# Two layer norms in one, a layer norm without a centring product, chained layer norms, and a segment pipeline one unit deeper

## The chip, the core and the metric

The kernel runs on one core of one Trainium2 chip. A core has five engines with queues of their own: TensorE (PE, matrix products; PEld are its weight loads), VectorE (DVE), ScalarE (ACT), GpSimd (POOL) and SyncE (SP, which here only starts DMAs). Each works its queue in order and waits on semaphores for the others. The metric is the device time of the whole program in microseconds (us).

## What is computed

Eight layers over the same tensor of 4 x 1024 tokens of 128 features (all in f32), each added to its input behind a plain layer norm:

```python
x = x + rwkv_moe(layernorm(x))       # its own first step is again a layer norm: _ln(., ln1_g, ln1_b)
x = x + ffn(layernorm(x))            # ends in layernorm(x + collapsed, gamma, beta)
x = x + favor(layernorm(x))
x = x + ffn(layernorm(x))
x = x + segment_attention(layernorm(x))
x = x + tree(layernorm(x))
x = x + lru(layernorm(x))
x = x + tree(layernorm(x))

def _layernorm(x, axis=-1, eps=1e-05):
    m = jnp.mean(x, axis=axis, keepdims=True)
    v = jnp.var(x, axis=axis, keepdims=True)
    return (x - m) / jnp.sqrt(v + eps)
```

In the feed-forward layer each token picks one of nine paths by a small score; `x` in `x + collapsed` is the layer's normed input. In the segment attention a token attends to its own segment of 64 and to every fourth token of four neighbouring segments.

## The kernel before

**Layout.** Features lie on the 128 partitions, the 4096 tokens on the free axis, cut in eight chunks (`NCH`) of 512 (`CH`). PSUM has eight banks of 128 x 512 f32 (`k.bank[0..7]`). The order on each engine is written out by hand, stage after stage. No scheduler moves anything.

**A layer norm** (class `Norm`, driven by `layernorm`) takes a chunk through five steps: `center` (PE, line 85: the product with `I - 1/128`, into bank c % 4), `square` (ACT, line 92), `variance` (PE, line 103: the mean over the partitions as a product, into banks 4 to 6, or 4 and 5 where `vary` is 2), `deviation` (ACT, lines 110 and 112: Ln, then Exp of minus one half), and `scale` (DVE: line 118 for a plain norm. With gain and bias it is 121 and 124, or 121 and 126 where the result is added to the residual). On PE the loop does `variance(c - 2)`, then `center(c)`, then whatever the stage feeds in. On ACT it does `square(c + 2)`, then `deviation(c)`. `center(c)` waits until `ln_out` shows that the chunk four back has been scaled, since it writes over that chunk's bank; the count runs on from norm to norm, so the next norm's chunk 0 waits for chunk 4 of this one.

**The start.** The input is loaded in rows, turned on PE (line 2224), copied to `X` by DVE (2178, the `keep` step), normed into `Y` (no gain), and normed again into `N` with `ln1_g` and `ln1_b`: two passes of eight chunks. The vectors of all layers arrive as rows in one small table, `vrows`, which PE turns at the end of the first pass and DVE copies to `vecs` (2248). POOL then folds three vectors into weights (192, 195), and `wkv` begins: its products (219, 220) on PE, copies out of PSUM on ACT (281), a scan on DVE (354).

**The feed-forward layer** (`feedforward`, called twice) takes chunk by chunk: `hidden` (PE 858, three products), `scores` (864), DVE's `choose` (804 to 812), `turned` (870), `spread` (878, the choice as three masks in banks 6, 7 and 4), DVE's `mask` (820), `down` (885, three products with `W2`) and DVE's `add` (825, the sum with the normed input, into `Z`). The last chunk's steps stand behind the loop, with three `center` products of the closing norm between them. Then comes that norm (gain, bias, residual, in place on `X`), and behind it the plain norm `X` to `Y` that begins the next layer. Only `center(0)` and `square(0)` of the second are drawn forward (`ahead`).

**The segment stage** (`segments`) works 64 units (`N`). For unit n: `scores` (PE 1830, into one of two pairs of banks), DVE's `maxima` (2009, 2010) and `shift` (2018, 2019), ACT's `exp` (1930), POOL's `halve` (1977), DVE's `sums` (2026, 2028), ACT's `weight` (1934, 1936), POOL's `weigh` (1982, 1983), PE's `turned` (1840), ACT's copy of it (1926), PE's `weighed` (1852). In PE's turn n stand `scores(n)`, `turned(n - 3)`, `weighed(n - 4)`, and then one of three things that share one bank, `other`: a `project` (1812), a `values` (1863) or an `output` (1870). Each waits (`free()`) until the last one's result was read out of `other`: by ACT for `project` (1908 or 1898) and `values` (1919), by DVE's `add` (2033, residual) for `output`. ACT's `heads` (1942) empties the bank of `weighed` every eight units. In each batch of 16 units `project` stands at 0, 1, 3, 4, 7 and 11, `values` at 2, 6, 10 and 14, `output` at 5 and 13 from unit 13 on.

## Time and profile before

| | us |
|---|---|
| median of three runs | 1274.57 |
| lowest and highest | 1271.35, 1275.83 |
| the profiled execution | 1270.62 |
| its span in the profile | 1268.9 |

| stretch of the span (us) | what runs |
|---|---|
| 0 to 46 | load, two layer norms |
| 46 to 424 | wkv, experts |
| 424 to 544 | feed-forward with its norms |
| 544 to 688 | favor |
| 688 to 809 | feed-forward with its norms |
| 809 to 1084 | segment attention |
| 1084 to 1269 | tree, lru, tree, store |

All times below count from the start of the span; 1.7 us of the run lie outside it. A row of the timeline gives the start, the time from start to end, and in brackets how long the engine had been idle and who ended that. Neighbouring instructions overlap a little, so the step from one start to the next is often less than the duration. An f32 product shows as two PE instructions. In a row of stretches PEclk is the clock granted to TensorE as a share of 2.4 GHz; its two levels are 2.4 and 1.2 GHz, so that 0.57 is a mix of both.

### The profile page before, as it was taken

Reading aid. Unit: us, or ns where it says so; the run is one execution under the profiler, and the core shown is the slowest. Engines: PE = TensorE matmul, PEld = TensorE weight load, DVE = VectorE, ACT = ScalarE, POOL = GpSimd, SP = SyncE. Lnnn points to the kernel's source line nnn. Section 1 sums busy time; section 2 is a strip of 40 time slices with the busy share of each in tenths; the row PEclk is TensorE's granted clock in tenths of the full one; section 3 lists DMA queues with packets and bytes.
Section 4 is the critical chain, followed back from the end, with each engine's and each line's share of the span. In section 5 each row is a group of like instructions: output and inputs, shape, how many; then the busy total and the mean of one; then the engine's idle time right before and its main releaser. Section 6 shows DMA issues by size and latency. Waiting matters only on the chain.

```text
span 1268.9 us, 20399 instructions
## 1 busy us (share of the span) xinstructions
PE 1153.0 (91%) x7516; PEld 637.1 (50%) x7516; DVE 923.8 (73%) x1508; ACT 831.1 (65%) x1324; POOL 207.0 (16%) x313
## 2 busy tenths in 40 slices
PE   8988899999999999889998899798989888898787
PEld 4333344444444344367765353366666666463345
DVE  3869688777777756557775675488999997477766
ACT  5868655565565744745576636667787876768684
POOL 1000000000000000000000000167778777000000
PEclk9999999999999989979999999878999999999899
DMA  6000112212121000000000000000000000000002
GB/s 168 1 1 0 46 58 67 62 59 67 59 63 62 8 1 0 10 1 2 2 1 1 1 0 9 1 1 2 2 2 3 9 7 2 10 0 1 0 1 67
DMA packets 26076, 27.16 MB, mean 21 GB/s; under 512 B 3885, under 2 KB 17024, under 8 KB 25984
## 3 DMA queue, kind: packets, MB, share of 16 engines
q1 hardware_dynamic: 25938, 25.92, 6.9%
q8 instruction: 59, 0.97, 0.3%
q14 instruction: 33, 0.27, 0.1%
q10 hardware_dynamic: 46, 0.01, 0.0%
HBM read 23.30 MB, written 2.62 MB: 20 GB/s over the span
## 4 chain that ended last, share of the span: by engine, by line
PE 61%; DVE 16%; ACT 13%; issue 7%; POOL 1%; DMA 0%; DVEq 0%; ACTq 0%
PE psum L655 8%; PE psum L644 8%; PE psum L85 5%; PE psum L647 4%; PE psum L885 3%; PE psum L858 3%; PE psum L1830 3%; PE psum L1499 3%; ACT ln_std L112 3%; ACT ln_std L110 2%; PE psum L103 2%; PE psum L1273 2%; DVE arena L2010 2%; DVE N L2019 2%; ACT ln_sq L92 2%
## 5 line engine op out<-in xcount | busy, mean ns | idle before, releaser
L683 ACT ACTIVATE arena<-psum 128x512 f32<-128x512 f32 x128 | 69.5, 594 | 112.9 <-PE psum L644 112.9
L644 PE MATMUL psum<-arena,weights 128*128 128x512 f32 x256 | 120.8, 594 | 1.7 <-DVE N L124 1.0
L655 PE MATMUL psum<-arena,weights 128*128 128x512 f32 x256 | 120.3, 592 | 0.0
L103 PE MATMUL psum<-ln_sq,mean 128*128 128x512 f32 x192 | 97.1, 600 | 2.8 <-ACT ln_std L110 1.5
L541 DVE SCALAR_TENSOR_TENSOR arena<-diff,vecs,N 128x512 f32<-128x512 f32 x128 | 95.2, 746 | 0.0
L1930 ACT ACTIVATE N<-N 128x1024 f32<-128x1024 f32 x64 | 67.8, 1059 | 38.3 <-DVE N L2019 37.8
L603 DVE SCALAR_TENSOR_TENSOR arena<-arena,psum 128x512 f32<-128x512 f32 x64 | 44.0, 688 | 61.1 <-PE psum L655 61.1
L92 ACT ACTIVATE ln_sq<-psum 128x512 f32<-128x512 f32 x96 | 56.1, 593 | 45.5 <-PE psum L85 45.5
L1840 PE MATMUL psum<-ident,N 128*128 128x128 f32 x512 | 72.7, 287 | 12.5 <-POOL N L1983 11.9
L1830 PE MATMUL psum<-arena 32*128 32x128 f32 x1024 | 78.8, 295 | 4.8 <-ACT arena L1898 4.8
L1830 PEld LDWEIGHTS psum<-arena 32*128 32x128 f32 x1024 | 66.1, 197 | 31.3 <-issue 14.8
L655 PEld LDWEIGHTS psum<-arena,weights 128*128 128x128 f32 x256 | 48.6, 190 | 61.2 <-issue 61.2
L644 PEld LDWEIGHTS psum<-arena,weights 128*128 128x128 f32 x256 | 48.0, 190 | 62.0 <-issue 57.6
L1926 ACT ACTIVATE arena<-psum 128x1024 f32<-128x1024 f32 x64 | 65.5, 1024 | 17.8 <-PE psum L1840 17.6
L85 PE MATMUL psum<-X,center 128*128 128x512 f32 x128 | 67.4, 621 | 4.9 <-DVE N L118 1.9
L110 ACT ACTIVATE ln_std<-psum,eps 128x512 f32<-128x512 f32 x96 | 65.2, 679 | 8.9 <-PE psum L103 8.9
L118 DVE TENSOR_TENSOR Y<-psum,ln_std 128x512 f32<-128x512 f32 x48 | 33.2, 692 | 51.1 <-ACT ln_std L112 51.1
L1840 PEld LDWEIGHTS psum<-ident,N 128*128 128x128 f32 x512 | 57.2, 145 | 22.4 <-POOL N L1983 16.4
L694 ACT ACTIVATE arena<-arena 128x1024 f32<-128x1024 f32 x64 | 68.3, 1067 | 0.0
L1983 POOL TENSOR_TENSOR N<-N,arena 128x512 f32<-128x512 f32 x64 | 67.7, 1058 | 0.0
L1982 POOL TENSOR_TENSOR N<-N,arena 128x512 f32<-128x512 f32 x64 | 66.7, 1043 | 2.1 <-ACT arena L1936 2.1
L647 PE MATMUL psum<-arena,weights 128*128 128x512 f32 x128 | 65.4, 592 | 0.0
(318 smaller groups left out, 2452.2 us busy)
## 6 DMA issues: line engine op xcount, KB each, us to landing
arena<-tw_rows SPq DMA_DIRECT2D x64, 256.0 KB, 3.2
out_dram<-arena SPq DMA_DIRECT2D x8, 256.0 KB, 3.6
arena<-in_L_attn_a_x_dram SPq DMA_DIRECT2D x3, 512.0 KB, 6.4
weights<-in_L_attn_a_eWk_dram SPq DMA_DIRECT2D x1, 1024.0 KB, 5.9
arena<-in_L_attn_a_x_dram SPq DMA_DIRECT2D x2, 256.0 KB, 3.3
weights<-in_L_attn_a_eWr_dram SPq DMA_DIRECT2D x1, 512.0 KB, 9.6
tw_rows<-arena SPq DMA_DIRECT2D x2, 128.0 KB, 2.7
tw_rows<-arena SPq DMA_DIRECT2D x1, 256.0 KB, 3.7
```

The lines of the kernel that those rows point to most:

```text
L85: self.nc.tensor.matmul(k.bank[c % W][:], k.center[:], self.src(c), start=True, stop=True).then_inc(k.ln_centered, 1)
L92: self.nc.scalar.activation(k.ln_sq[:, c % W, :], k.bank[c % W][:], ACT.Square).then_inc(k.ln_squared, 1)
L103: self.nc.tensor.matmul(k.bank[W + c % self.vary][:], k.mean[:], k.ln_sq[:, c % W, :], start=True, stop=True).then_inc(k.ln_var, 1)
L110: self.nc.scalar.activation(k.ln_std[:, c % W, :], k.bank[W + c % self.vary][:], ACT.Ln, bias=k.eps[:, 0:1]).then_inc(k.ln_logs, 1)
L541: op = nc.vector.scalar_tensor_tensor(mixed[:, n % 4, a, :], k.diff[:, q % 2, :], k.vec((f"cm_k{e}", f"cm_r{e}")[a]), before, ALU.mult, AL ...
L644: op = nc.tensor.matmul(k.bank[2 * (n % 2) + h][:], k.eWk[:, e, h * P:(h + 1) * P], mixed[:, n % 4, 0, :], start=True, stop=True)
L647: nc.tensor.matmul(k.bank[6][:], k.eWr[:, e, :], mixed[:, n % 4, 1, :], start=True, stop=True).then_inc(k.ex_r, 1)
L655: op = nc.tensor.matmul(k.bank[4 + n % 2][:], k.eWv[:, e, h, :], ks[:, (2 * (n % 2) + h) * CH:(2 * (n % 2) + h + 1) * CH], start=(h == 0), ...
L683: op = nc.scalar.activation(kr[:, h * CH:(h + 1) * CH], k.bank[2 * (n % 2) + h][:], ACT.Relu)
L694: nc.scalar.activation(ks[:, n % 2 * 2 * CH:(n % 2 + 1) * 2 * CH], kr, ACT.Square).then_inc(k.ex_sq, 1)
L1830: op = nc.tensor.matmul(scored[half][:, e * P:(e + 1) * P], k.sg_Q[b % 2][at, seg, 2 * j:2 * j + 2, :].rearrange("p h n -> p (h n)"), k.sg ...
L1840: op = nc.tensor.transpose(turned_to[:, e * P:(e + 1) * P], pr[n % 4][:, e * P:(e + 1) * P], k.ident[:])
```

## The change

**1. The first two norms in one** (`TwoNorms`). After the first norm the features of a token have mean zero and variance v / (v + eps), so the second norm's factor is `(v (1 + eps) + eps^2)^(-1/2)` of the same centred value. There is one pass instead of two: PE centres and takes the variance once, ACT does two Ln and two Exp from the same bank, and DVE writes both `N` (with gain, then bias) and `Y`. `ln1_g` and `ln1_b` leave the table of rows and are loaded by themselves as columns, 128 x 1 each, first on ACT's queue. The table is turned in PE's turn 5 and copied after chunk 3 of the pass.

**2. The closing norm of the feed-forward layer without centring** (`CentredNorm`). The rows of `W2` (with `b2`) are made mean-free once, by DVE at the end of the norm ahead of the first feed-forward layer (two reductions, two small and three 128 x 128 operations), so `Z` has mean zero by itself. POOL squares each chunk of `Z` when `add` has written it. PE takes the mean of that into one of the banks 0, 1, 2, 0, 6, 7, 4, 5, and DVE scales from `Z` in SBUF. `center` and `square` are gone.

**3. The pair chained.** The next norm's `center(c)` for the first four chunks waits only for chunk c of the closing norm. Three of its `center` and two of its `square` stand inside the closing pass.

**4. Segments.** `turned` and `weighed` come one unit later on PE and ACT, `output`, `heads` and DVE's `add` too, `values` one unit earlier, and one `project` at 2 instead of 1.

```diff
+class TwoNorms(Norm):
+    def deviation(self, act, c):
...
+        act.wait_ge(k.ln_var, self.n0 + c + 1)
+        var = k.bank[W + c % self.vary][:]
+        nc.scalar.activation(k.ln_std[:, at, :], var, ACT.Ln, bias=k.eps[:, 0:1])
+        nc.scalar.activation(k.ln_std2[:, at, :], var, ACT.Ln, scale=1.0 + EPS_LN, bias=k.eps_eps[:, 0:1]).then_inc(k.ln_logs, 1)
+        act.wait_ge(k.ln_logs, self.n0 + c + 1)
+        nc.scalar.activation(k.ln_std[:, at, :], k.ln_std[:, at, :], ACT.Exp, scale=-0.5)
+        nc.scalar.activation(k.ln_std2[:, at, :], k.ln_std2[:, at, :], ACT.Exp, scale=-0.5).then_inc(k.ln_rstd, 1)
+    def scale(self, dve, c):
...
+        nc.vector.scalar_tensor_tensor(out, bank, k.ln1[:, 0:1], k.ln_std2[:, at, :], ALU.mult, ALU.mult).then_inc(k.ln_scaled, 1)
+        nc.vector.tensor_tensor(self.dst(c), bank, k.ln_std[:, at, :], ALU.mult)
+        dve.wait_ge(k.ln_scaled, self.second0 + c + 1)
+        nc.vector.tensor_scalar(out, out, k.ln1[:, 1:2], None, ALU.add).then_inc(k.ln_out, 1)
+class CentredNorm(Norm):
+    SPOTS = (0, 1, 2, 0, 6, 7, 4, 5)
+    def variance(self, pe, c):
...
+        pe.wait_ge(k.ff_sq, self.squared0 + c + 1)
+        self.enter(pe, c)
+        self.nc.tensor.matmul(k.bank[self.SPOTS[c]][:], k.mean[:], self.squares(c), start=True, stop=True).then_inc(k.ln_var, 1)
+    def scale(self, dve, c):
...
+        nc.vector.scalar_tensor_tensor(self.src(c), self.src(c), k.vec(self.gain), k.ln_std[:, c % W, :], ALU.mult, ALU.mult).then_inc(k.ln_scaled, 1)
+        nc.vector.scalar_tensor_tensor(self.residual(c), self.src(c), k.vec(self.bias), self.residual(c), ALU.add, ALU.add).then_inc(k.ln_out, 1)
...
-        pe.wait_ge(k.ln_out, self.n0 + c + 1)
+        pe.wait_ge(k.ln_out, self.n0 + c + 1 - (self.chained if c < W else 0))
...
+        if self.chained and c < W:
+            act.wait_ge(k.ln_out, self.n0 + c + 1)
...
+        for c in range(NCH):
+            pool.wait_ge(k.ff_z, PRIMED["ff_z"] + base + c + 1)
+            nc.gpsimd.tensor_tensor(after.squares(c), after.src(c), after.src(c), ALU.mult).then_inc(k.ff_sq, 1)
...
+        after.scale(dve, 0)
+        after.scale(dve, 1)
         mask(B - 1, 1)
+        add(B - 1, 0)
+        after.scale(dve, 2)
         add(B - 1, 1)
...
-    PROJ = {0: 0, 1: 1, 3: 2, 4: 3, 7: 4, 11: 5}
+    PROJ = {0: 0, 2: 1, 3: 2, 4: 3, 7: 4, 11: 5}
...
-        return n // 4 if n < N and n % 4 == 2 else None
+        return n // 4 if n < N and n % 4 == 1 else None
...
-        return (n - 13) // 8 if n >= 13 and n % 8 == 5 else None
+        return (n - 14) // 8 if n >= 14 and n % 8 == 6 else None
...
-            if 0 <= n - 3 < N:
-                turned(n - 3)
             if 0 <= n - 4 < N:
-                weighed(n - 4)
+                turned(n - 4)
+            if 0 <= n - 5 < N:
+                weighed(n - 5)
```

**ACT in the first pass.** Before: squares, then one Ln and one Exp for a chunk (the pass follows twice in this form).

```order
L92 ACTIVATE ln_sq<-psum 128x512 x3
L110 ACTIVATE ln_std<-psum,eps 128x512
L112 ACTIVATE ln_std<-ln_std 128x512
L92 ACTIVATE ln_sq<-psum 128x512
L110 ACTIVATE ln_std<-psum,eps 128x512
L112 ACTIVATE ln_std<-ln_std 128x512
```

Now, once (`eps_eps` is the constant eps squared, `arena` here holds the second factor):

```order
L94 ACTIVATE ln_sq<-psum 128x512 x3
L149 ACTIVATE ln_std<-psum,eps 128x512
L150 ACTIVATE arena<-psum,eps_eps 128x512
L152 ACTIVATE ln_std<-ln_std 128x512
L153 ACTIVATE arena<-arena 128x512
L94 ACTIVATE ln_sq<-psum 128x512
L149 ACTIVATE ln_std<-psum,eps 128x512
```

A chunk has four such operations and a square instead of, over both passes, four and two squares; the dependent passes have become one.

**PE at the end of the feed-forward layer.** Before: from behind the last `scores` (L864) over three `center` of the closing norm to its first `variance`.

```order
L85 MATMUL psum<-arena,center 128x512
L870 MATMUL psum<-ident,arena 9x128 x4
L85 MATMUL psum<-arena,center 128x512
L878 MATMUL psum<-arena,spread 128x512 x3
L85 MATMUL psum<-arena,center 128x512
L885 MATMUL psum<-arena,ffw 128x512 x3
L133 UNCONDITIONAL_BRANCH
L103 MATMUL psum<-ln_sq,mean 128x512 x2
```

Now, from the same place (L192 is the variance of the closing norm, L87 the next norm's `center`, from `X`):

```order
L192 MATMUL psum<-arena,mean 128x512 x2
L974 MATMUL psum<-ident,arena 9x128 x4
L990 MATMUL psum<-arena,ffw 128x512 x3
L982 MATMUL psum<-arena,spread 128x512 x3
L192 MATMUL psum<-arena,mean 128x512 x2
L990 MATMUL psum<-arena,ffw 128x512 x3
L219 UNCONDITIONAL_BRANCH
L192 MATMUL psum<-arena,mean 128x512
L87 MATMUL psum<-X,center 128x512
L192 MATMUL psum<-arena,mean 128x512
L87 MATMUL psum<-X,center 128x512
```

Four variances now stand ahead of the last `down`, and the two norms alternate behind it.

**PE in the segment stage, units 13 to 16.** Before: `output`, then the turns of 14 (with `values`), 15 and 16 (with `project`).

```order
L1870 MATMUL psum<-arena,weights 128x512
L1830 MATMUL psum<-arena 128x128 x8
L1840 MATMUL psum<-ident,N 128x128 x8
L1852 MATMUL psum<-arena,ln_sq 32x64 x16
L1863 MATMUL psum<-ident,arena 128x128 x4
L1830 MATMUL psum<-arena 128x128 x8
L1840 MATMUL psum<-ident,N 128x128 x8
L1852 MATMUL psum<-arena,ln_sq 32x64 x16
```

Now, from `values` in turn 13 (L1970) to the end of turn 15: L1937 is `scores`, L1947 `turned`, L1959 `weighed`, L1977 `output`.

```order
L1970 MATMUL psum<-ident,arena 128x128 x4
L1937 MATMUL psum<-arena 128x128 x8
L1947 MATMUL psum<-ident,N 128x128 x8
L1959 MATMUL psum<-arena,ln_sq 32x64 x16
L1977 MATMUL psum<-arena,weights 128x512
L1937 MATMUL psum<-arena 128x128 x8
L1947 MATMUL psum<-ident,N 128x128 x8
L1959 MATMUL psum<-arena,ln_sq 32x64 x16
```

Behind `output` there was a `values` one turn later; now the next user of `other` is the `project` of turn 16, or of turn 7 in a batch that has one there.

## Rows read from the trace of the kernel before

**Rows 1.** Page, part 1: busy us, share of the span, instructions.

```profile
PE 1153.0 (91%) x7516; PEld 637.1 (50%) x7516; DVE 923.8 (73%) x1508; ACT 831.1 (65%) x1324; POOL 207.0 (16%) x313
```

**Rows 2.** Stretches: us, busy us by engine (instructions), PEclk, DMA share, GB/s.

```profile
12.00:46.00 34.00, 31.84 (x85) 13.52 (x84) 18.29 (x33) 28.45 (x49) 3.14 (x14) 1.00 0.33 91
500.00:546.00 46.00, 38.07 (x96) 15.35 (x95) 25.00 (x47) 30.32 (x51) 1.88 (x11) 1.00 0.03 7
820.00:840.00 20.00, 16.63 (x84) 10.95 (x84) 14.08 (x25) 10.10 (x19) 6.93 (x9) 0.57 0.00 1
840.00:1076.00 236.00, 204.48 (x3544) 158.50 (x3544) 213.05 (x370) 186.49 (x348) 181.92 (x208) 0.98 0.02 4
```

**Rows 3.** Timeline: ACT in the first two passes, and DVE's first scan.

```profile
13.05 0.68 ACT L110 ACTIVATE ln_std<-psum,eps 128x512 f32<-128x512 f32 x1
...
22.92 0.58 ACT L92 ACTIVATE ln_sq<-psum 128x512 f32<-128x512 f32 x1
...
23.40 0.68 ACT L110 ACTIVATE ln_std<-psum,eps 128x512 f32<-128x512 f32 x1
24.11 0.63 ACT L112 ACTIVATE ln_std<-ln_std 128x512 f32<-128x512 f32 x1
...
24.65 0.67 ACT L110 ACTIVATE ln_std<-psum,eps 128x512 f32<-128x512 f32 x1
...
43.91 0.63 ACT L112 ACTIVATE ln_std<-ln_std 128x512 f32<-128x512 f32 x1
...
47.13 2.29 DVE L354 TENSOR_TENSOR_SCAN arena<-diff,arena 128x1024 f32<-128x1024 f32 x1 [0.16 <-ACT arena L281]
```

**Rows 4.** Timeline, second pass: from a factor to the square four chunks on.

```profile
30.98 0.63 ACT L112 ACTIVATE ln_std<-ln_std 128x512 f32<-128x512 f32 x1
...
31.65 0.75 DVE L121 SCALAR_TENSOR_TENSOR N<-psum,vecs,ln_std 128x512 f32<-128x512 f32 x1 [3.59 <-ACT ln_std L112]
...
32.44 0.49 DVE L124 TENSOR_SCALAR N<-N,vecs 128x512 f32<-128x512 f32 x1
...
34.14 0.60 ACT L92 ACTIVATE ln_sq<-psum 128x512 f32<-128x512 f32 x1 [0.80 <-PE psum L85]
```

**Rows 5.** Timeline: end of both feed-forward layers, first scale of the second norm.

```profile
499.22 1.05 PE L864 MATMUL psum<-Wo,arena 64*128 64x9 f32 x8
...
506.59 2.74 PE L885 MATMUL psum<-arena,ffw 128*128 128x512 f32 x6
...
529.57 0.69 DVE L118 TENSOR_TENSOR Y<-psum,ln_std 128x512 f32<-128x512 f32 x1 [1.84 <-ACT ln_std L112]
...
796.98 0.69 DVE L118 TENSOR_TENSOR Y<-psum,ln_std 128x512 f32<-128x512 f32 x1 [1.84 <-ACT ln_std L112]
```

**Rows 6.** Page, part 5: a product of two 128 x 512 tiles on POOL.

```profile
L1982 POOL TENSOR_TENSOR N<-N,arena 128x512 f32<-128x512 f32 x64 | 66.7, 1043 | 2.1 <-ACT arena L1936 2.1
```

**Rows 7.** Timeline, inside the feed-forward loop: DVE's mask.

```profile
461.78 1.88 DVE L820 TENSOR_TENSOR arena<-arena,psum 128x512 f32<-128x512 f32 x3 [0.57 <-PE psum L878]
```

**Rows 8.** Timeline, segment stage: units 18 to 20 and 23, and what preceded.

```profile
895.92 0.69 DVE L2009 TENSOR_REDUCE arena<-psum 128x8 f32<-128x512 f32 x1
...
899.37 0.68 DVE L2009 TENSOR_REDUCE arena<-psum 128x8 f32<-128x512 f32 x1
...
899.93 1.12 ACT L1919 ACTIVATE ln_sq<-psum,weights 128x128 f32<-128x128 f32 x4
...
903.37 0.69 DVE L2009 TENSOR_REDUCE arena<-psum 128x8 f32<-128x512 f32 x1 [0.48 <-PE psum L1830]
...
914.59 0.66 PE L1863 MATMUL psum<-ident,arena 128*128 128x128 f32 x4 [1.76 <-DVE X L2033]
...
916.38 0.69 DVE L2009 TENSOR_REDUCE arena<-psum 128x8 f32<-128x512 f32 x1 [0.93 <-PE psum L1830]
```

**Rows 9.** Waits of 820 to 1076: total us, times, longest.

```profile
DVE arena L2009 <- PE psum L1830: 23.0, 30, 3.4
```

**Rows 10.** Timeline, end of the segment stage: the last `weighed`.

```profile
1081.44 0.65 PE L1852 MATMUL psum<-arena,ln_std 128*32 128x64 f32 x32
```

More of the change, by code:

```diff
@@ L165, in first @@
     def first(pe, c):
-        if c == NCH + 1:
-            after.center(pe, 0)
+        if 6 <= c < 9:
+            after.center(pe, c - 6)
     def turned(act, c):
-        if c == NCH - 2:
-            after.square(act, 0)
+        if c in (5, 6):
+            after.square(act, c - 5)
     return first, lambda dve, c: None, turned
@@ L703, in stage_rwkv @@
 def stage_rwkv(nc, k, block, a, feed, norms):
-    first, second, third, after = norms
+    first, second, after = norms
     layernorm(k, block, first, feed)
@@ L707, in stage_rwkv @@
     ffn_loads(k, block, a)
-    layernorm(k, block, second)
-    wkv(nc, k, block, a, third)
-    experts(nc, k, block, lambda feed: layernorm(k, block, third, feed), after)
+    wkv(nc, k, block, a, second)
+    experts(nc, k, block, lambda feed: layernorm(k, block, second, feed), after)
 FFN_GROUPS = ((0, 2), (2, 6), (6, 9))
@@ L832, in turn @@
                 choose(it, c)
-                if not (first and c == 0):
+                if not (first and c == 0 or last and c == 1):
                     add(*before)
@@ L886, in down, with turn @@
             op.then_inc(k.ff_out, 1)
-        def turn(it, first):
+        def turn(it, first, last=False):
             for c in range(2):
@@ L901, in turn @@
                 scores(it, c)
-                if not (first and c == 0):
+                if not (first and c == 0 or last and c == 1):
                     down(*before)
         turn(0, True)
-        with pe.Fori(1, B) as it:
+        with pe.Fori(1, B - 1) as it:
             turn(it, False)
-        for c in range(3):
-            pe.wait_ge(k.ff_hid, 3 * (base + NCH - 1) + c + 1 + PRIMED["ff_hid"])
-            after.center(pe, c)
-            if c == 0:
-                turned(B - 1, 1)
-            if c == 1:
-                spread(B - 1, 1)
+        turn(B - 1, False, True)
+        after.variance(pe, 0)
+        after.variance(pe, 1)
+        turned(B - 1, 1)
+        down(B - 1, 0)
+        spread(B - 1, 1)
+        after.variance(pe, 2)
+        after.variance(pe, 3)
         down(B - 1, 1)
@@ L944, in _ @@
         activations(act, k, "natural_log_exp_and_others")
-        after.square(act, 0)
+        after.deviation(act, 0)
         choice(B - 1, 1)
-        for c in range(1, 3):
-            after.square(act, c)
+        for c in range(1, 4):
+            after.deviation(act, c)
 def stage_ffn(nc, k, block, norms):
@@ L954, in stage_ffn @@
     k.ff_calls += 1
+    after.chained = NCH - W
     feedforward(nc, k, block, call, lambda feed: layernorm(k, block, first, feed), second)
@@ L1948, in _ @@
                 queries(k.bank[4 + c], 0, c, part)
-        for n in range(N + 6):
-            if n >= 12 and n % 8 == 4:
-                heads((n - 12) // 8)
-            if 0 <= n - 3 < N:
-                turned(n - 3)
+        for n in range(N + 7):
+            if n >= 13 and n % 8 == 5:
+                heads((n - 13) // 8)
+            if 0 <= n - 4 < N:
+                turned(n - 4)
             if n < N:
@@ L2046, in _ @@
                 shift(n)
-            if n >= 14 and n % 8 == 6:
-                add((n - 14) // 8)
+            if n >= 15 and n % 8 == 7:
+                add((n - 15) // 8)
             if n >= 1:
```

148 lines of the change are left out of this document (112 added, 36 removed).

## The prediction

> **What bounds the kernel now.** I read the page's busy line first [rows 1]: PE is busy 91% of the span, so no other engine can be the bound everywhere, but the average hides stages with other limits. So I went on to the stretches [rows 2]. From 12 to 46 us, PE is busy 31.8 of 34.0 us and ACT 28.5. In the pair of norms after a feed-forward layer (500 to 546) it is 38.1 and 30.3 of 46. In the segment stage (840 to 1076) DVE has 213.1 of 236.0 and PE 204.5. In the norm passes no engine is full: each chunk runs PE, ACT, PE, ACT, DVE, and the bank that it holds comes free at the end. There I followed the timeline from one chunk to the next [rows 3 to 5]. In the segment stage I followed DVE's first reduction from unit to unit and read what it waited for [rows 8, 9].
>
> **Part 1, the first two norms in one.** In the pass of before, ACT takes 0.48 us from a square to the Ln behind it (22.92 to 23.40), 0.71 from Ln to the Exp that needs it (to 24.11) and 0.54 to the next instruction [rows 3]. Of two Ln in a row none shows the step; I take 0.57, between the square's 0.48 and the full 0.68. A chunk on ACT is then 0.48 + 0.57 + 0.71 + 0.54 + 0.54 = 2.84 us. The bank's cycle is longer. Before, an Exp ends at 30.98 + 0.63 = 31.61 and the square that waits for this chunk's bank (through DVE's 121, 124 and a `center`) starts at 34.14: 2.53 us [rows 4]. DVE now has one more operation between these two. Before, 124 starts 0.79 behind 121, since it needs its result; now two steps between independent operations lie there. Three masks take 1.88 us, so such a step is 0.60 [rows 7]; the one with gain is longer by 0.06, so I take 0.67 + 0.61. That is 0.49 more, 3.02 us. From that square to the end of the second Exp it is 0.48 + 0.57 + 0.71 + 0.54 + 0.63 = 2.93, so two chunks take 5.95. The first Ln stays at 13.05 [rows 3], and its factors end at 15.5. By the cycle the factors of chunks 1 to 5 end near 18.3, 21.4, 24.3, 27.4 and 30.3. The last two chunks need no square and take 2.36 each, so the last ends at 35.0. Before it was 43.91 + 0.63 = 44.54 [rows 3]. DVE's last scale is now 0.5 us longer and stands ahead of its first scan, so the scan gains 9.1 instead of 9.5: from 47.13 to 38.0. PE's first products of `wkv` wait for POOL's fold. The vectors are copied behind chunk 3, near 24.3 + 2 us, and the fold is POOL's 3.1 us of that stretch [rows 2], so they start near 30, with 5 us to spare. The two 128 x 1 loads have no like in the trace. They can cost nothing or, in front of the first input load, up to 1 us; I take 0.5. **Part 1: 8.6 us, bounds 6 and 10.**
>
> **Parts 2 and 3, the pair of norms.** PE's last `scores` start at 499.22 and are through at 500.2 [rows 5]. From there PE has, in order, two variances (0.86 each: the six instructions at 506.59 take 2.74, that is 0.43 apart), `turned` 0.43, `down` 2.58, `spread` 0.65, two variances and `down`: 9.7 us, ending at 509.95. Before, the last `down` began at 506.59 [rows 5] and was through 2.58 us later, so this piece is 0.8 us longer. DVE's two scales ahead of `mask` (1.5 us each) fit, since `mask` waits for `spread` anyway. POOL needs 1.04 us for a square, by its products of the same size [rows 6]. The last but one is there long before its variance; the last is ready near 512. Then PE alternates variance and `center`, seven products of 0.86 to 516.0. ACT with 1.25 us for a chunk (0.71 + 0.54) and two squares between ends its last factor at 517.6. Then come `square(2)`, Ln and Exp of the next norm's chunk 0, to 519.3, and DVE's first `scale` of that norm starts at 519.35. Before it was 529.57 [rows 5]: 10.2 us. From there on the second norm has the same steps and the same bank cycle as before. The second feed-forward layer has the same times shifted by 267.4 us (529.57 and 796.98 [rows 5]), so it gains the same. The fold of `W2` is seven DVE operations of a quarter or half of 128 x 512, at most 7 x 0.25 us by the 0.69 of a whole one. DVE then waits for the first `scores` of the layer, which covers them, so I cost the fold at nothing; without that cover it costs 1.7 us once. **Parts 2 and 3: 20.4 us, bounds 12 and 23.** The lower bound is the removed work alone, 0.86 us of PE for seven centrings a pass, without the chaining.
>
> Inside the feed-forward loop POOL's square runs beside DVE's mix of the next chunk. In the trace of before DVE has a wait of 0.57 us ahead of `mask` there [rows 7], and a product of `down` takes 0.86 us against 0.60 for a mask, so a late start of the masks is partly caught up. Even if a square held DVE up by its whole 1.04 us, most of it would fall into these gaps.
>
> No row shows what a POOL product does to a DVE operation with two inputs in SBUF. The Trainium skill, SBUF — State Buffer, section SBUF: two separate sides, says that the two engines share a pair of ports as an exclusive lock, taken by a DVE operation with two SBUF inputs against a POOL operation that reads SBUF. By it a square and the mix, or a square and a scale of the closing norm, would run one after the other.
>
> **Part 4, the segments.** With nothing to wait for, a unit takes DVE 3.45 us (895.92 to 899.37 [rows 8]). DVE waits for `scores` 23.0 us in all, 3.4 of it at the first unit [rows 9]: 19.6 us are there to be had. Two kinds make up most of it. Seven times the wait is 0.93 (at unit 23 [rows 8], and at 15, 31, 39, 47, 55 and 63): PE holds a `values` until DVE's `add` has read `other` (1.76 us idle at 914.59), and the next `scores` are queued behind it. The other kind follows a `values` copied by ACT (899.93 to 901.05 [rows 8]): the `project` of the next turn waits for it, and `scores` come 0.48 late (903.37); with ACT's `heads` there too I count 0.6. After the change `output` stands one turn later and the next user of `other` two or more turns on, except in the two batches where `project` stands at 7 right behind it (units 23 and 39). There the wait stays and gets longer by the difference of a `project` (0.86 and its filling, say 1.1) and a `values` (0.66 [rows 8]), to about 1.4 us. At the other five the 0.93 goes, but `values` now stands one turn ahead of each of the seven `output`, so 0.5 comes in its place. I count for after: 7 x 0.5 before `output`, 2 x 0.5 where `project` follows `values` at 17 and 33, 2 x 0.6 with `heads`, 2 x 1.4, and about 4 in the first 16 units, where the clock was 0.57 in the stretch 820 to 840 [rows 2]: 12.5 us against 19.6, so 7.1. Waits of PE for POOL before `turned` go too, but they only matter through these. At the end the last `weighed` starts at 1081.44 [rows 10], after two `center` of the next norm. These now come ahead of it, since ACT's copy is late anyway; 1.3 us. One price is new: DVE's `shift(n)` now waits for `turned(n - 4)` of the same turn. Four transposes take 0.66 us [rows 8], so the eight of `turned` end about 1.2 us after `scores(n)`, and `shift` starts behind two reductions of 0.68, 1.3 after them. At half clock it would be late by about 0.8 us a unit. **Part 4: 8.3 us, bounds 0 and 12.**
>
> **The sum.** 8.6 + 20.4 + 8.3 = 37.3. Against the profiled execution that is 1270.6 - 37.3 = 1233.3. That run lies 4 us under the median of the three, so for a median I predict **1237 us**, 2.9% less. A measurement here tells apart about 0.3%.
>
> **The rivals.** (a) *The deeper segment pipeline gives nothing*: the wait of `shift` for `turned`, and longer waits at `project`, eat part 4. For: DVE is 90% busy there, and only 0.1 to 0.3 us separate `turned` from `shift`. Against: five of the seven long waits lose their cause. It gives 1274.6 - 29.0 = 1246; chance 0.12. (b) *The pairs gain only the removed centring*: the chain then ends in ACT or DVE as before, with 12 instead of 20.4: also 1246; chance 0.08. (c) *POOL's squares hold DVE up*: 16 squares of 1.04 us [rows 6], none of them hidden, are 16.6 us: 1254. Against it are the gaps above; chance 0.08. This is the skill's rule on the shared ports carried to its end. (d) *Slower than before*: the segment stage falls to 1.2 GHz. PE's 204.5 us at 0.98 [rows 2] would take 401 us at half clock, so a us spent there loses about 0.4. Before, PE was at the low level for part of 820 to 840 only [rows 2]. With 120 us at the low level the loss is 49 and the time 1286. It decides from about 91 us on. The change leaves PE's work in the stage the same and its pauses shorter, so I give it 0.03. (e) *The merged norm is bound by something I don't see* (the column loads, the clock with a less busy PE): part 1 at 0 gives 1246; chance 0.05.
>
> **How the numbers follow.** The forecast as summed has 0.64. Its own bounds, with 4 us for where the clock's low stretches fall, are 1229 to 1243. The range must take in (a), (b) and (e), so it runs from 1228 to 1250 and leaves out (c), (d) and the low tail of the forecast. Faster by over 0.3%: all but (d), 0.97, of which I take 0.01 for cases that fall together; same 0.01, slower 0.03.
>
> **What would show it.** The first scan of `wkv` near 38 us and ACT without idle time before. The first plain scale 10 us earlier after each feed-forward layer, PE alternating variance and `center` without gaps. In the segment stage DVE's waits for `scores` about 12 to 13 us beyond the first one, none of 0.93 at units 15, 31, 47, 55 and 63, and long ones at 24 and 40. It would be wrong if DVE's mixes in the feed-forward loop took longer than before, if `shift` idled for `turned`, or if the low clock covered more of 820 onward.

## The result, and the profile after

The changed kernel takes **1257.0 us** (median of four executions; 1255.5 to 1258.7) against 1274.7 before (1271.4 to 1275.8, with a fourth execution beside the three above). The ratio is 0.9866, with a 95% interval from 0.984 to 0.989: 1.3% less, where I had forecast 2.9% (1237) and a range up to 1250. The profiled execution took 1258.3 us, with a span of 1256.2.

Of the page of after, the busy line (us, share of the span, instructions) and TensorE's granted clock in 40 slices; the first answers to [rows 1].

```profile
PE 1139.7 (91%) x7444; PEld 639.9 (51%) x7452; DVE 930.1 (74%) x1515; ACT 815.3 (65%) x1300; POOL 230.7 (18%) x330
...
PEclk9999999999999989989999999698899988999899
```

The changes ahead of the segments show in five rows of the timeline (start, duration): the scan, and in each feed-forward layer the first hidden product (L962) and the first plain scale (L122). They answer to the scan in [rows 3] and the first plain scales in [rows 5].

```profile
38.08 2.29 DVE L440 TENSOR_TENSOR_SCAN arena<-diff,arena 128x1024 f32<-128x1024 f32 x1
...
434.68 3.37 PE L962 MATMUL psum<-arena,ffw 128*128 128x512 f32 x6
...
512.84 0.69 DVE L122 TENSOR_TENSOR Y<-psum,ln_std 128x512 f32<-128x512 f32 x1 [0.18 <-ACT ln_std L116]
...
692.93 3.37 PE L962 MATMUL psum<-arena,ffw 128*128 128x512 f32 x6
...
769.84 0.69 DVE L122 TENSOR_TENSOR Y<-psum,ln_std 128x512 f32<-128x512 f32 x1 [0.19 <-ACT ln_std L116]
```

The first scan is 9.05 us earlier. From a layer's first hidden product to the first plain scale it takes 78.2 and 76.9 us. Before it took 88.4 and 87.2, from these products to the scales of [rows 5]:

```profile
441.15 1.02 PE L858 MATMUL psum<-arena,ffw 128*128 128x512 f32 x2
...
709.80 1.71 PE L858 MATMUL psum<-arena,ffw 128*128 128x512 f32 x3
```

Both pairs gained 10.3.

The segment stage shows the rest. First its stretches (columns as in [rows 2]; the last one runs from the first unit's maxima to the last unit's), then waits of 797 to 1053.7 (us in total, times, longest), the first of which answers to [rows 9].

```profile
795.00:815.00 20.00, 17.41 (x91) 11.31 (x92) 13.07 (x23) 7.89 (x18) 7.55 (x10) 0.50 0.00 0
815.00:1059.00 244.00, 215.06 (x3456) 167.34 (x3456) 212.54 (x369) 183.74 (x343) 177.89 (x204) 0.91 0.01 4
...
797.61:1053.64 256.03, 227.13 (x3451) 174.16 (x3452) 220.54 (x382) 188.02 (x353) 181.89 (x209) 0.88 0.01 4
```

```profile
DVE arena L2116 <- PE psum L1937: 31.2, 31, 3.4
...
PE psum L1959 <- ACT arena L2049: 9.9, 7, 2.4
PE psum L1947 <- ACT arena L2033: 7.3, 9, 1.7
...
DVE N L2125 <- PE psum L1947: 5.7, 9, 0.7
...
PE psum L1919 <- DVE X L2140: 3.5, 2, 1.8
```

TensorE's waits before, in the same stretch (824.8 to 1067.97), were longest for DVE's `add` and for GpSimd's weights:

```profile
PE psum L1863 <- DVE X L2033: 12.4, 7, 1.8
PE psum L1840 <- POOL N L1983: 10.1, 17, 1.2
PE psum L1852 <- ACT arena L1942: 4.1, 7, 1.1
```

DVE waits 31.2 us for scores where it waited 23.0, and 5.7 us more in its shift for `turned`. TensorE's waits for `add` fell from 12.4 us to 3.5, as meant, but all its waits in the stretch are 28.8 us in 29 times against 30.1 in 43: fewer, longer and for other engines. The mean granted clock is 0.88. Before, the same stretch was 243.2 us long with a granted clock of 0.96. At two levels, 0.88 over 256 us is about 61 us at 1.2 GHz; the clock records say 62.4, before 21.5.

The table takes each kernel apart, profiled executions all. "Low" is the time at 1.2 GHz in the stretch ahead of it, from the clock records. P is the start of the stage's first projections, D from the first unit's maxima to the last one's, tail from there to the last `add`, rest to the end of the span.

| kernel | median us | P | low | P to maxima | D | low | tail | rest |
|---|---|---|---|---|---|---|---|---|
| before | 1274.7 | 809.6 | 35.0 | 15.2 | 243.2 | 21.5 | 16.1 | 184.9 |
| after | 1257.0 | 782.4 | 41.9 | 15.2 | 256.0 | 62.4 | 17.3 | 185.3 |
| e1_turns_as_before | 1246.0 | 776.9 | 27.3 | 14.0 | 251.7 | 44.2 | 17.6 | 186.3 |
| e2_turns_alone | 1285.2 | 809.6 | 35.0 | 15.2 | 256.0 | 62.4 | 17.3 | 184.7 |
| e3_heads_first | 1247.2 | 780.0 | 38.5 | 15.2 | 248.7 | 58.9 | 17.3 | 185.1 |
| e4_centre_last | 1253.0 | 779.9 | 35.1 | 15.2 | 256.0 | 62.4 | 17.7 | 184.5 |
| e5_slots_alone | 1245.9 | 782.8 | 41.9 | 15.2 | 245.2 | 35.1 | 18.1 | 185.4 |
| e6_fill_start | 1250.1 | 779.7 | 34.1 | 11.4 | 254.4 | 54.6 | 17.3 | 184.7 |
| e7_heads_centres | 1247.9 | 776.9 | 31.7 | 15.2 | 249.2 | 55.5 | 15.6 | 186.4 |
| e8_squares_act | 1259.1 | 783.0 | 41.9 | 15.2 | 255.9 | 62.4 | 17.3 | 185.3 |
| e9_all_mended | 1231.4 | 779.7 | 34.1 | 11.4 | 239.2 | 17.1 | 14.0 | 184.8 |
| e10_fill_before | 1268.9 | 809.4 | 34.1 | 11.4 | 243.0 | 20.5 | 17.7 | 186.2 |
| e11_heads_centres | 1242.1 | 780.3 | 38.5 | 15.2 | 248.0 | 45.3 | 14.1 | 186.0 |
| e12_deep_mended | 1240.0 | 779.9 | 37.5 | 11.4 | 242.6 | 34.1 | 15.6 | 185.6 |

P varies by 5.9 us among the seven kernels whose code is the same up to there (after, e1, e3, e4, e5, e7 and e11: 776.9 to 782.8), and it roughly follows the low time ahead of it (27.3 to 41.9). Most of the spread lies between the first scan and the first hidden product: 392.3 us with none of it low in e7, 393.7 with 3.4 in e4, 396.6 with 10.2 in after; before it was 394.0 with 3.4. At an equal low time nothing is lost there, so the fold of `W2`, which the prediction costed at nothing, costs nothing. The sum predicted 809.6 - 29.0 = 780.6. The profiled run of after lies near the late end of that spread.

### The profile page after: what moved, and what is told of

It is laid out like the page before. It is cut to its first block, busy times and chain, and to the rows that moved or that the text cites. A ratio compares the mean times of both kernels' runs of the same rounds, so it can differ in the third digit from the quotient of the medians.

```text
span 1256.2 us, 20246 instructions
## 1 busy us (share of the span) xinstructions
PE 1139.7 (91%) x7444; PEld 639.9 (51%) x7452; DVE 930.1 (74%) x1515; ACT 815.3 (65%) x1300; POOL 230.7 (18%) x330
## 4 chain that ended last, share of the span: by engine, by line
PE 63%; DVE 17%; ACT 14%; issue 6%; DMA 0%; SPq 0%; DVEq 0%; ACTq 0%
PE psum L730 8%; PE psum L741 8%; PE psum L733 4%; PE psum L990 3%; PE psum L87 3%; PE psum L1937 3%; PE psum L962 3%; PE psum L1606 3%; PE psum L1947 2%; PE psum L1380 2%; DVE N L2126 2%; ACT ln_std L116 2%; ACT ln_std L114 2%; DVE arena L2117 2%; DVE arena L2116 2%
## 5 line engine op out<-in xcount | busy, mean ns | idle before, releaser
L1937 PE MATMUL psum<-arena 32*128 32x128 f32 x1024 | 84.6, 310 | 4.8 <-ACT arena L2005 4.8
L1937 PEld LDWEIGHTS psum<-arena 32*128 32x128 f32 x1024 | 71.1, 210 | 33.7 <-issue 18.7
L1947 PE MATMUL psum<-ident,N 128*128 128x128 f32 x512 | 77.2, 299 | 10.2 <-ACT arena L2033 9.9
L730 PEld LDWEIGHTS psum<-arena,weights 128*128 128x128 f32 x256 | 48.6, 192 | 62.4 <-issue 58.0
L105 PE MATMUL psum<-ln_sq,mean 128*128 128x512 f32 x144 | 73.2, 601 | 3.1 <-ACT arena L150 1.1
L87 PE MATMUL psum<-X,center 128*128 128x512 f32 x128 | 67.0, 618 | 6.5 <-DVE N L165 3.2
L1947 PEld LDWEIGHTS psum<-ident,N 128*128 128x128 f32 x512 | 61.2, 152 | 20.0 <-issue 15.1
L2116 DVE TENSOR_REDUCE arena<-psum 128x8 f32<-128x512 f32 x64 | 43.9, 687 | 31.3 <-PE psum L1937 31.2
L1775 DVE TENSOR_REDUCE arena<-psum 128x32 f32<-128x1024 f32 x32 | 39.2, 1224 | 32.8 <-PE psum L1606 32.8
L2084 POOL TENSOR_TENSOR mixed<-N 128x256 f32<-128x256 f32 x64 | 46.5, 727 | 74.4 <-ACT N L2037 74.3
## 6 DMA issues: line engine op xcount, KB each, us to landing
arena<-tw_rows SPq DMA_DIRECT2D x64, 256.0 KB, 3.1
out_dram<-arena SPq DMA_DIRECT2D x8, 256.0 KB, 3.6
arena<-in_L_attn_a_x_dram SPq DMA_DIRECT2D x2, 256.0 KB, 4.1
tw_rows<-arena SPq DMA_DIRECT2D x1, 256.0 KB, 3.4
```

Of the source, the lines that this page charges most:

```text
L87: self.nc.tensor.matmul(k.bank[c % W][:], k.center[:], self.src(c), start=True, stop=True).then_inc(k.ln_centered, 1)
L105: self.nc.tensor.matmul(k.bank[W + c % self.vary][:], k.mean[:], k.ln_sq[:, c % W, :], start=True, stop=True).then_inc(k.ln_var, 1)
L730: op = nc.tensor.matmul(k.bank[2 * (n % 2) + h][:], k.eWk[:, e, h * P:(h + 1) * P], mixed[:, n % 4, 0, :], start=True, stop=True)
L1937: op = nc.tensor.matmul(scored[half][:, e * P:(e + 1) * P], k.sg_Q[b % 2][at, seg, 2 * j:2 * j + 2, :].rearrange("p h n -> p (h n)"), k.sg ...
L1947: op = nc.tensor.transpose(turned_to[:, e * P:(e + 1) * P], pr[n % 4][:, e * P:(e + 1) * P], k.ident[:])
L2116: nc.vector.tensor_reduce(mx[n % 2][:, 0:8], mine, AX.X, ALU.max)
```

## Which part loses

**Part 4 taken out, and part 4 alone.** The edit of the first run, on the changed kernel (the second makes the same change, reversed, on the kernel before):

```diff
-            if 0 <= n - 4 < N:
-                turned(n - 4)
-            if 0 <= n - 5 < N:
-                weighed(n - 5)
+            if 0 <= n - 3 < N:
+                turned(n - 3)
+            if 0 <= n - 4 < N:
+                weighed(n - 4)
...
```

with `heads` and the turns of `project`, `values`, `output` and `add` as before.

> The changed kernel with the segment stage's turns put back as they were (part 4 undone, parts 1 to 3 kept). By the traces the stage starts 27.2 us earlier than before at its first maxima, and the store is only 13.3 earlier, so 13.9 us are lost behind it. If the new turns cause the loss (queue theory), units 0 to 63 take again the 243.2 us they took before and the tail its 16.0, and the time is 1275 - 27 = 1247 us, within 3; DVE's waits for the scores are again about 23 us in 30. If instead the loss comes from TensorE's clock in the earlier start, whatever the turns (clock theory), the stage stays at about 256 us and the time at 1255 to 1258.

> The kernel before with part 4 alone. Queue theory: 12.8 us more between the first and the last unit and 1.3 more in the tail, so about 1289 us (1284 to 1292), with the new wait for `turned` in DVE's shift and waits of some 2 us at units 14, 30, 46 and 62. Clock theory: the stage as before, or up to 8 us shorter as I predicted, 1266 to 1276 us.

Without part 4: **1246.0 us** (ratio 0.9765, 0.974 to 0.979). Part 4 alone: **1285.2 us** (1.0088, 1.006 to 1.011). Part 4 costs about 11 us on either base by the medians, and the executions of the kernels compared don't overlap (1241.8 to 1248.6 against 1255.5 to 1258.7, and 1283.9 to 1287.6 against at most 1277.0 beside them). Its stretch D is 256.0 us both times, with 62.4 us at the low clock both times, though it starts 27 us apart. So what falls low there goes with the order of the work more than with the place in time. But the order of before isn't fixed at 243.2 either: in e1 the same order took 251.7 us with 44.2 us low, and DVE waited 31.1 us in 37 for scores, where I expected 23 in 30. Its 22.7 us more of low clock cost 8.6, 0.38 for each. So in the profiled executions part 4 adds 12.8 us to D against the kernel before, but only 4.3 against e1: how large its loss is depends on the low clock in the kernel that it is set beside.

**The places alone.** The depth of three and four turns and `heads` as before, the new turns of `project`, `values`, `output` and `add` kept:

```diff
-            if 0 <= n - 4 < N:
-                turned(n - 4)
...
+            if 0 <= n - 3 < N:
+                turned(n - 3)
...
```

> The changed kernel with `turned` and `weighed` three and four turns behind as before, and `heads` where it was, but with the new turns of `project`, `values`, `output` and `add`. It splits part 4 in two: the run without part 4 took 1246 us, the changed kernel 1257. If the depth of the pipeline carries the loss (its `heads` standing behind the second half of `queries`), this kernel is at 1243 to 1248; if the new places of `project` and `values` carry it, at 1253 to 1258.

**1245.9 us** (0.9775, 0.975 to 0.981). The loss is in the depth, not in the places; but the places bring nothing by the medians either (e1: 1246.0), though they take the wait for `add` away here too (3.5 us in 2). D fell by 10.8 us to 245.2, with 35.1 us low (PEclk 0.93 in the row of its stretch), and TensorE again waits for GpSimd's weights, now its longest sum:

```profile
797.95:1043.13 245.18, 218.60 (x3491) 166.52 (x3492) 220.47 (x383) 189.34 (x354) 181.88 (x209) 0.93 0.01 4
```

```profile
PE psum L1947 <- POOL N L2090: 8.1, 12, 1.6
PE psum L1959 <- ACT arena L2049: 6.4, 5, 1.8
```

In after, the wait for GpSimd's weights is gone, as meant. But the transposes have one place in PSUM, so `turned` of one unit now waits for ACT's copy of the last one (7.3 us in 9), and `weighed` for `heads` (9.9 in 7, where it was 4.1 in 7 before).

## The queues

**`heads` behind `queries`.** In after, `weighed(8t + 8)` needs the bank that ACT's `heads` empties. TensorE's rows around unit 14, and ACT's:

```profile
847.59 1.06 PE L1947 MATMUL psum<-ident,N 128*128 128x128 f32 x8 [0.83 <-ACT arena L2033]
850.75 1.08 PE L1959 MATMUL psum<-arena,ln_sq 128*32 128x64 f32 x32 [2.10 <-ACT arena L2049]
851.76 1.12 PE L1970 MATMUL psum<-ident,arena 128*128 128x128 f32 x4
852.81 2.08 PE L1937 MATMUL psum<-arena 32*128 32x128 f32 x16
```

```profile
848.55 0.24 ACT L2043 ACTIVATE arena<-arena 128x40 f32<-128x40 f32 x1
848.69 1.43 ACT L2005 ACTIVATE arena<-psum,weights 128x512 f32<-128x512 f32 x2
850.01 0.59 ACT L2049 ACTIVATE arena<-psum 128x512 f32<-128x512 f32 x1
```

`heads` (L2049) stands behind the second half of `queries` (L2005, two copies, 1.43 us together). `weighed` idles 2.10 us, the scores queued behind it start late and at half clock (2.08 instead of 1.16 us), and DVE waits 3.43 us at unit 14. It waits 1.90, 2.14 and 1.94 at units 30, 46 and 62. TensorE waits 2.39 and 2.10 us for `heads` at 30 and 46, again behind `queries`. At 62 it waits 1.95, but there `heads` follows `exp` and `weight`, with no `queries` ahead: that wait is not explained by this order.

```diff
-            if n >= 13 and n % 8 == 5:
-                heads((n - 13) // 8)
...
             if 0 <= n - 1 < N:
                 weight(n - 1)
+            if n >= 12 and n % 8 == 4:
+                heads((n - 12) // 8)
```

> The changed kernel, with ScalarE's `heads` moved from the start of iteration 8t+13 to the end of iteration 8t+12, ahead of the second half of `queries`. If the waits of about 2 us at units 14, 30, 46 and 62 come from `heads` standing behind `queries` (queue theory), three of them (14, 30, 46: the last unit has no queries) lose 1.5 to 2 us each and the low clock that follows them, another 1 to 2 us each: 1247 to 1252 us. If they are only where the clock happens to be low, the time stays within 2 us of 1257.

**1247.2 us** (0.978, 0.975 to 0.982), 9.9 less than after by the medians. In the profile D is 7.3 us shorter with only 3.5 us less at the low clock, so some 6 us of it are the waits themselves. The units 14, 30 and 46 now wait 2.33, 0.96 and 0.96 us, and the sum behind `heads` fell from 9.9:

```profile
PE psum L1959 <- ACT arena L2049: 2.7, 4, 0.8
```

**The `center` products in the last turns.** After's end of the stage on TensorE:

```profile
1061.01 1.99 PE L87 MATMUL psum<-X,center 128*128 128x512 f32 x4
1062.83 1.04 PE L1947 MATMUL psum<-ident,N 128*128 128x128 f32 x8
...
1064.38 1.98 PE L87 MATMUL psum<-X,center 128*128 128x512 f32 x4
1066.20 1.04 PE L1947 MATMUL psum<-ident,N 128*128 128x128 f32 x8
```

Each pair of `center` (L87) holds a `turned` (L1947) for 1.8 us.

```diff
-            if n in (N + 1, N + 2):
-                pe.wait_ge(k.sg_arg, n - 2)
-                for c in range(2 * (n - N - 1), 2 * (n - N)):
+            if n in (N + 4, N + 5):
+                pe.wait_ge(k.sg_arg, n - 5)
+                for c in range(2 * (n - N - 4), 2 * (n - N - 3)):
```

> The changed kernel, with the two pairs of `center` of the next norm moved from TensorE's turns 65 and 66 to turns 68 and 69, behind the last `weighed`. In the changed kernel the last `turned` starts 12.6 us after the last maxima, before it was 10.0. Queue theory: the four products (1.0 to 1.2 us a pair, twice) no longer stand ahead of the last two `turned`, the last `add` comes 1.5 to 2.5 us earlier, about 1255 us. Rival: GpSimd's last weights are what the last `turned` waits for, and nothing changes (1257).

**1253.0 us** (0.983, 0.979 to 0.987), and no gain where I looked for it. The last `turned` starts 10.3 us after the last maxima instead of 12.6, but the `center` products now stand ahead of `output` (L1977), for which the last `add` waits; the tail is 17.7 us against 17.3:

```profile
1064.19 3.70 PE L87 MATMUL psum<-X,center 128*128 128x512 f32 x8
1067.72 1.02 PE L1977 MATMUL psum<-arena,weights 128*128 128x512 f32 x2
```

The median is 4 us lower, of which the profile shows 2.5 as an earlier P; its four executions spread over 9 us (1250.2 to 1259.0). So I put them where TensorE idles anyway:

```diff
+            if n == N:
+                pe.wait_ge(k.sg_arg, N - 1)
+                after.center(pe, 0)
+                after.center(pe, 1)
+            if n in (N + 1, N + 2):
+                pe.wait_ge(k.sg_arg, N)
+                after.center(pe, n - N + 1)
```

> The kernel with `heads` ahead of the second half of `queries` (1247.2 us), and with the next norm's four `center` spread over the last turns: two at turn 64, where TensorE waits 2.0 us for the copy of the turned unit, and one each at turns 65 and 66, where it waits 0.6. Queue theory: the last `turned` starts 10.3 us after the last maxima instead of 12.6 and the last `add` still 4.75 behind it, so 2.2 us less, 1245 us. Rival: the end of the stage is set by the chain of copies alone and the time stays at 1247.

**1247.9 us** (0.979, 0.975 to 0.984). The tail is 15.6 us instead of 17.3, near the 2.2 expected; the median can't tell that from e3's, whose runs spread over 8 us. That spread is wider than what this edit gives.

## The clock

TensorE waits 3.4 us ahead of the stage's first projections and 4.75 us behind them. In after the projections took 8.3 us, and units 0 to 4 ran at half clock. Idle products fill the two pauses, on the changed kernel and on the one before:

```diff
+        def fill(count):
+            for _ in range(count):
+                nc.tensor.matmul(other[:], k.center[:], k.X[:, 0:CH], start=True, stop=True)
...
             pe.wait_ge(k.sw_in, 7 * 16)
+            fill(3)
             pe.wait_ge(k.ln_out, normed)
...
         first()
+        fill(4)
```

> The changed kernel with idle products on TensorE, whose result nobody reads: three of 128x512 ahead of the segment stage's first projections, where TensorE waits 3.4 us, and four behind them, where it waits 4.75 us. Queue theory alone: the waits are covered by other work and nothing gets shorter, 1257 us (or up to 3 longer, if a filler still runs when its wait ends). Clock theory: the granted clock of the first projections and of units 0 to 8 stays at 2.4 instead of 1.2 GHz; the projections take 4.2 instead of 8.3 us and the units that wait for scores lose 1 to 1.5 us less each, 1245 to 1250 us.

> The kernel before with the idle products alone. Before, too, TensorE waits 3.4 us ahead of the stage's first projections and the clock is at 1.2 GHz in units 0 to 4. Clock theory: the first scores come 3 to 4 us earlier and 1 to 2 us of the first units' waits go, 1269 to 1271 us. If the idle products only shift the low stretches, 1273 to 1275.

**1250.1 us** (0.982, 0.978 to 0.985) and **1268.9 us** (0.9952, 0.994 to 0.997): 6.9 and some 6 us less. One of the six executions of e10 took 6426 us, which nothing here explains; without it the median is 1268.8. The rows of e6 (the idle products are L1911):

```profile
776.25 2.74 PE L1911 MATMUL psum<-X,center 128*128 128x512 f32 x6
779.72 5.42 PE L1918 MATMUL psum<-Y,weights 128*128 128x512 f32 x12 [0.74 <-DVE Y L122]
784.98 3.60 PE L1911 MATMUL psum<-X,center 128*128 128x512 f32 x8
789.90 1.16 PE L1942 MATMUL psum<-arena 32*128 32x128 f32 x16 [1.32 <-ACT arena L2011]
```

The six projections take 5.4 us, the first scores 1.16 instead of 2.08, and the first maxima come 11.4 us after P instead of 15.2. That is a gain from work that nobody needs. The rest of e6 lies in D (1.6) and ahead of P (2.7), which is the spread of P.

## The squares on GpSimd

In both closing norms ACT takes the squares of the last two chunks, where it idles, and GpSimd the other six:

```diff
-        for c in range(NCH):
+        for c in range(NCH - 2):
             pool.wait_ge(k.ff_z, PRIMED["ff_z"] + base + c + 1)
...
+    def own_square(self, act, c):
+        act.wait_ge(self.k.ff_z, self.z0 + c + 1)
+        self.nc.scalar.activation(self.squares(c), self.src(c), ACT.Square).then_inc(self.k.ff_sqa, 1)
```

> The changed kernel with the squares of the last two chunks of both feed-forward norms taken by ScalarE (which idles there) instead of GpSimd. In the changed kernel the two VectorE additions (both operands and result in SBUF) that run beside these squares took 1.41 us instead of 0.75. If that is a lock between the two engines, they take 0.75 again, and with VectorE on the path the time falls by 1.3 us a norm, 2.6 in all, 1254.5 us; if the additions are not on the path, 1257. If the lengthening has another cause, they stay at 1.41.

Rows of after, GpSimd's square and the two VectorE operations beside it, then the addition in e8:

```profile
501.88 0.74 DVE L210 SCALAR_TENSOR_TENSOR arena<-arena,vecs,ln_std 128x512 f32<-128x512 f32 x1
502.04 1.48 POOL L893 TENSOR_TENSOR arena<-arena 128x512 f32<-128x512 f32 x1 [11.05 <-DVE arena L925]
502.66 1.41 DVE L212 SCALAR_TENSOR_TENSOR X<-arena,vecs,X 128x512 f32<-128x512 f32 x1
```

```profile
503.17 0.75 DVE L220 SCALAR_TENSOR_TENSOR X<-arena,vecs,X 128x512 f32<-128x512 f32 x1
```

The addition is back at 0.75 us, so the 1.41 came from the square beside it. The median is **1259.1 us** (0.988, 0.983 to 0.993), no better than after, where 2.6 us less were expected. Its executions spread over 11 us, but the profile agrees: from the first hidden product to the first plain scale it takes 78.2 us as in after. Inside the feed-forward loop, too, the mixes beside a square took 1.22 us instead of 0.75, six of them in the first layer. They fell into VectorE's waits: the two pairs gained 10.3 us each all the same.

The Trainium skill, SBUF — State Buffer, section SBUF: two separate sides, says that the pair of ports goes to whichever of the two operations starts first, for its whole length. The trace agrees in both directions, if not to the full length: the square (1.04 us alone), begun 0.58 us before a scale's end, took 0.44 longer, and the addition, begun 0.86 before the square's end, took 0.66 longer.

## Everything mended, at either depth

The best version takes the places of part 4, the old depth, `heads` ahead of the first half of `queries` (iteration 8t + 11), the first three `center` in TensorE's wait of turn 64 with the fourth behind the last `weighed`, and the idle products; e11 leaves these out.

```diff
             if 0 <= n - 1 < N:
                 weight(n - 1)
+            if n >= 11 and n % 8 == 3:
+                heads((n - 11) // 8)
...
+            if n == N:
+                pe.wait_ge(k.sg_arg, N)
+                for c in range(3):
+                    after.center(pe, c)
+            if n == N + 3:
+                after.center(pe, 3)
```

> Parts 1 to 3, the new places of `project`, `values`, `output` and `add`, the old depth of three and four turns, and three more edits: `heads` at the end of iteration 8t+11, ahead of the first half of `queries`; the next norm's `center` of chunks 0 to 2 at the end of turn 64, where TensorE waits 2.7 us for GpSimd's weights, and that of chunk 3 behind the last `weighed`; and the idle products at the stage's start. From the run with the new places alone (1245.9 us): heads 1 to 2 us (0.9 us of wait at units 13, 29 and 45), the tail 4 us (the pairs of `center` took 3.5 and 2.0 us there ahead of turned(63) and weighed(63)), the idle products 5.4 us as they gained at the stage's start in their own run: 1235 us. If the clock takes its low stretches elsewhere instead, 1239 to 1242.

> The same without the idle products: 1240 to 1241 us by the queues alone (1245.9 less 4 in the tail and 1 to 2 for heads). If the tail's length is set by GpSimd's weights and not by the `center` products ahead of turned(63), 1244.

**1231.4 us** (0.968, 0.966 to 0.970) and **1242.1 us** (0.974, 0.973 to 0.976). Both are faster than the changed kernel; e9 is also faster than the run without part 4 (1246.0, 0.974 to 0.979), while e11's interval overlaps that one's. The tail is 14.0 and 14.1 us, 4 less than in e5, as expected. The idle products gave 10.7 us where I expected 5.4, since D shrank too: 239.2 us with 17.1 low against 248.0 with 45.3, that is 0.31 for each us at the low clock. The two profiled executions are e9's fastest and e11's slowest (1231.1 and 1245.6), so the profile shows more than the medians.

The twin of e9 at the changed kernel's depth is e7 with the idle products. It is no exact twin: its `heads` stands ahead of the second half of `queries`, and two `center` stand in turn 64 and one each in 65 and 66.

> The changed kernel at its own depth of four and five turns, with everything mended beside it: `heads` ahead of the second half of `queries`, the `center` products in TensorE's waits of the last turns, and the idle products at the stage's start. It asks whether the deeper pipeline is worth anything once nothing else is in its way; its twin at the old depth took 1231.4 us. My prediction's step (the depth shortens the waits for scores by 7 us) would give 1225 to 1228. If the depth brings nothing, 1230 to 1234. If the depth itself costs (the copy of the turned unit, the shift's wait for `turned` and one more unit to drain), 1236 to 1243; from the run with `heads` and `center` mended (1247.9) less the 5.4 us that the idle products gained, 1242.

**1240.0 us** (0.972, 0.969 to 0.975), 8.6 above its twin by the medians and 6.1 in the profile. Its four executions lie in two groups (1237.3 and 1237.4, 1242.6 twice), like e9's five (1231.1 to 1231.4, 1235.8 and 1236.4), and group against group the distance is some 6 us. Of the 6.1, 3.5 are in D, 1.6 in the tail, where one more unit has to be drained, 0.8 in the rest. The stretch D of e9, then of e12, and what TensorE waits for most in each:

```profile
791.05:1030.21 239.16, 210.94 (x3491) 161.25 (x3492) 220.05 (x383) 189.03 (x354) 181.99 (x209) 0.96 0.02 4
```

```profile
791.27:1033.90 242.63, 215.91 (x3451) 165.59 (x3452) 220.01 (x382) 187.41 (x353) 182.17 (x209) 0.93 0.01 4
```

```profile
PE psum L1952 <- POOL N L2098: 9.2, 17, 1.6
```

```profile
PE psum L1952 <- ACT arena L2042: 8.1, 10, 1.7
PE psum L1964 <- ACT arena L2058: 5.3, 5, 1.9
```

The deeper order waits for other engines and hardly less: TensorE's waits in D are 26.7 us in 33 times, in e9 28.0 in 46. VectorE's own work is the same 220 us. TensorE has 17 us more at the low clock. At 0.31 these cost 5.3, more than the 3.5 by which D is longer, so at an equal clock the deeper order would be some 2 us shorter. That is an estimate. What in the deeper order brings the clock down (fewer but longer pauses would fit) wasn't tried by itself and stays open.

## Why the prediction was wrong

- **Part 1** (8.6 us, that is 9.1 less 0.5 for the column loads): right. The scan came 9.05 us earlier. TensorE's first transposes came at 4.56 instead of 4.10, and ACT then took 21.97 us from the first Ln (13.47) to the end of the last factor, where I had summed 21.95 (13.05 to 35.0). That the total is so close is in part luck: in the seven kernels with the same code up to there the scan came between 36.7 and 38.4, always 24.6 behind the first Ln, so the gain is 8.7 to 10.4.
- **Parts 2 and 3** (20.4): right, 10.3 a pair against 10.2, with variance and `center` alternating as foreseen. Rival (b) falls. DVE's mixes beside a square took longer, which I had named as a sign of being wrong; it cost nothing, since they fell into waits.
- **Parts 1 to 3 together**: the run without part 4 took 1246.0 us; 1274.6 less 29.0 is 1245.6. So close a match is luck: in its profiled execution P came 32.7 us earlier, and D was 8.6 longer. In the profiled run of after 27.2 of the 29.0 were there at P, with 41.9 us low ahead of it against 35.0 before.
- **Part 4** (8.3; its terms 7.1 and 1.3 make 8.4) is the step that failed, by its sign: it cost about 11 us by the medians and 14.1 in the profile, 12.8 in D and 1.2 in the tail. The count of waits "12.5 us against 19.6" came to 27.8. It was made at full clock, with "about 4 in the first 16 units"; these alone waited 10.8 us beyond the first, and before they had waited 8.5. Where the clock was high some of the count held: unit 24 waited 1.40, as forecast (unit 40 1.91), and unit 55 0.36 instead of 0.93. Missing were three things. The waits at 14, 30 and 46 from `heads` behind `queries` (about 6 us by e3) I had put at 0.6 for two of them. The waits of TensorE for GpSimd's weights were not removed but exchanged for waits for ACT's copy. And the low clock lasted 40.9 us longer in D, which at 0.31 to 0.38 is 13 to 16 us. As an estimate the account closes: D came out 19.9 us above the forecast (12.8 longer instead of 7.1 shorter), and `heads` (less the 1.2 it had there) and the clock make 17 to 20 of it. What makes the clock fall more in this order stays open.
- **The tail**: I took 1.3 us of gain because the `center` products would come ahead of the last `weighed` in ACT's shadow. They came ahead of the last two `turned` and held them: 1.2 us of loss. Placed in real pauses they were worth 1.7 (e7).
- **The shift's wait for `turned`** came as priced, in all nine cases at the low clock, 0.34 to 0.68 us each, 5.7 us in sum.
- **Rival (a)**, a part 4 that gives nothing, was too mild. **Rival (c)**, the lock, exists but is covered: nothing that could be measured, not 16.6. **Rival (d)** had the right mechanism and price (0.4 per us) at the wrong size. I asked only whether the stage would fall low altogether, and took "its pauses shorter" as a reason against: they became fewer and longer. I had also misread [rows 2]: before, the clock wasn't low in 820 to 840 only, but also for 10 us of 840 to 1076, whose PEclk is 0.98. It fell low for 41 us more, and this term of middling size was not in the sum, and in the range with 4 us only.

## What to carry over

A step that is moved a turn later in one queue must be looked up in every queue that it hands work to: here one copy of 0.6 us behind two others of 1.4 together, on an engine that was 73% busy, stopped TensorE three times for over 2 us. Count the waits that take the place of those removed, and give the clock a term of its own between none and all: its low time times the loss per us (0.31 to 0.38 here). Where TensorE must pause ahead of a dense stage, products that nobody reads can be cheaper than the pause.

## What was unexpected of the hardware

- One and the same order of the segment stage took 243.2 or 251.7 us, with 21.5 or 44.2 us at 1.2 GHz; the code ahead of P, equal in seven kernels, ended over a spread of 5.9 us. Yet the deeper order had 62.4 us low in each of four kernels (after, e2, e4 and e8).
- The clock fell in a stretch in which no single wait of TensorE after the first scores exceeded 2.4 us. The Trainium skill, TensorE: Matmul & The Clock Gate, section A second HAM failure mode: psum-queue depth-cycling, describes a kernel in which short idle times between groups of products let the clock swing between its levels; this trace agrees in that the clock was low eight separate times in D, 62.4 us in all, but no run here shows that the short waits bring it down.
- Seven idle products of about 0.9 us each, in pauses of 3.4 and 4.75 us, made the kernel before 6 us faster, the changed one 6.9 and the mended one 10.7.
